# The closing work of each batch row, moved to other steps of the attention schedule (one core, Trainium2)

## The chip, the cores and the metric

The kernel runs on one core of one Trainium2 chip. The metric is the device time of one execution in microseconds, lower is better. The engines are named as the profile names them: PE is TensorE (matmuls and transposes), DVE is VectorE, ACT is ScalarE, POOL is GpSimd, SP is SyncE, which here only issues DMAs. All five run their own instruction streams in order and meet at semaphores only.

## The reference, cut to what matters

Four layers are computed one after the other on a tensor of 4 x 1024 x 256: a gated linear attention, a mixture of experts, a differential attention, and a second mixture of experts. Each is followed by a residual add and a layer norm. The change lies in the third layer:

```python
q1, q2 = (q[..., :hd], q[..., hd:])          # 16 heads of 16, two score maps each
s1 = jnp.einsum('bhqd,bhkd->bhqk', q1, k1) * scale
s2 = jnp.einsum('bhqd,bhkd->bhqk', q2, k2) * scale
a1 = jax.nn.softmax(causal s1);  a2 = jax.nn.softmax(causal s2)
out = jnp.einsum('bhqk,bhkd->bhqd', a1 - lam * a2, v)
rms = jnp.mean(out * out, axis=-1, keepdims=True)
out = out * jax.lax.rsqrt(rms + EPS) * head_norm_w * (1.0 - LAMBDA_INIT)
return out.transpose(0, 2, 1, 3).reshape(B, S, D) @ Wo.T + bo
...
x = _layernorm(x + _L1_attn_ref(x, ...), axis=-1)
```

So after the heads of one batch row b are done, what remains for that row is: square, mean over each head, inverse root, scale, transpose, one product with Wo, add to the residual x, and a layer norm. I call this the closing work of the row.

## The kernel before, in words

The attention stage (`attention`, L1735) handles 4 batch rows x 8 groups of two heads, 32 rounds `w` in all, with `b, g = w // 8, w % 8`. Every round has 24 steps `s`. What each engine does in a step is one string of letters in `STEPS` (L1776), and every engine walks the same generator `steps()` (L1806), picking out its own letters; so the order on each engine is fixed when the program is built. The letters that matter:

- `s`: scores of one block of keys, PE (L2359) into one of three single PSUM banks 4, 5, 6, two banks a step, then ACT's exponentials (L2063), one per bank. Blocks with few columns (steps 4, 6, 20, 22) pack two heads' maps in a bank, and the odd step after them has no scores.
- `m`: a part of the row maxima of a later round. PE (L2297, L2302) fills a pair of banks and DVE reduces it (L2158). Two bank pairs (0-1 and 2-3) take turns (`turn`, L1846). 19 of these a round, none in steps 1, 5, 6, 8, 15, 17 and 21 to 23.
- `v`: PE's products of exponentials and values (L2277).
- `h`, `H`, `d`: in step 4, PE transposes the heads of the round before (L2230) into one of the two bank pairs, ACT copies them out (L2102), and DVE takes the reciprocal of the denominators (L2108).
- `r`: in step 15, PE transposes the maxima (L2330), ACT copies them (L2040) and POOL splits them (L1985).
- `x`: POOL zeroes the upper triangle of a diagonal block (L1995), in steps 2, 7, 11 (twice), 21, 22, 23 (twice); the products of that block wait for it.
- `end`: the end of a step. The closing work of row b is spread over the ends of steps in the eight rounds after it, by small tables that map (round modulo 8, step) to a part. Row 3's closing work comes after the last round and is not governed by the tables.

The tables and what they place are these. `squared`: POOL squares one of eight parts (L1969), in steps 13 to 20 of round 0. `meant`: DVE's sums over heads (L2175), steps 18, 20, 22 of round 0 and step 0 of round 1. `all_squared`: ACT's inverse root of them (L80 and L82, `roots`), which waits for all four sums. `scaled`: POOL's multiplication of one of eight parts (L1974), which waits for the root. `joined`: PE transposes four blocks (L2312) into one single bank, ACT copies it (L2047). `put_out`: PE's fp32 product with Wo (L2323) into one single bank. `added`: DVE adds that bank to x (L2182) and takes the layer norm's statistics (L70, L74). `rooted`: ACT's inverse root of the variances (L80, L82). `normed`: DVE applies mean and root (L2195).

A part that needs a single bank takes the next of the three in turn, between the scores of the step before and the step after (`single`, L1841). PE writes the third bank after it only when its reader, ACT or DVE, has released it. In rounds 30 and 31 PE also multiplies weight matrices for the last layer (L2338) at the ends of steps 14 to 17 and 19 to 22 of round 30 and 5 to 8 and 12 to 15 of round 31, and DVE splits the results (L2169, L2171); there are no maxima of a later round left there.

The code rows around the tables:

Of the kernel before, what the change touches and what calls it, by code (L numbers as in the profile page):

```python
# [1734 lines left out]
def attention(nc, A, K, PS, D, own, before, keep):  # L1735
# [57 lines left out]
    exps_to = lambda m: first_exp[12] * (m // 12) + first_exp[m % 12]  # L1793

    biased = 14
    joined = {(1, 14): 0, (2, 3): 1, (2, 9): 2, (2, 15): 3}
    put_out = {(3, 14): 0, (4, 14): 1, (5, 14): 2, (6, 14): 3}
    added = {(3, 15): 0, (4, 15): 1, (5, 15): 2, (6, 15): 3}
    rooted = {(4, 19): 0, (6, 19): 1}
    normed = {(4, 23): 0, (5, 3): 1, (6, 23): 2, (7, 3): 3}  # L1800
    squared = {(0, 13 + i): i for i in range(8)}
    scaled = {(1, s): i for i, s in enumerate((5, 6, 8, 9, 13, 14, 15, 16))}
    all_squared = (1, 3)
    meant = {(0, 18): 0, (0, 20): 1, (0, 22): 2, (1, 0): 3}

    def steps():  # L1806
# [866 lines left out]
def program(nc, A, out):  # L2673
    with ExitStack() as ctx:
# [30 lines left out]
        st_rope = rope(nc, A, K, PS, D, own, st_moe)  # L2705
        late = ExitStack()
        st_att, parts = attention(nc, A, K, PS, D, own, st_rope, late)
        st_mix = mix(nc, A, K, PS, D, own, out, parts, late)
        stages = (st_gla, st_moe, st_rope, st_att, st_mix)
# [111 lines left out]
```

How the kernel before makes its waits and increments, by code:

```python
def clear(e, K, bank, stage):  # L49
    e.wait_ge(K.left, 5 * stage)
    n = [s.num for s in bank]
    e.sem_clear(range(n[0], n[-1] + 1)).then_inc(K.cleared, 1)
# [13 lines left out]
def layernorm_stats(e, step, ST, MV, tiles):  # L67
    for i, t in enumerate(tiles):
        n = step.on(e.bn_stats(ST[:, i, :], t))
        first = n if i == 0 else first
    for i in range(len(tiles)):
        e.wait_ge(step.sem, first + i)
        a = e.bn_aggr(MV[:, i, :], ST[:, i, :])
    return a
# [2 lines left out]
def rsqrt(e, step, K, dst, src, tmp, scale, col):  # L78
    n = step.on(e.activation(tmp, src, ACT.Ln, bias=K.EPS[:, col:col + 1], scale=scale))
    e.wait_ge(step.sem, n)
    return e.activation(dst, tmp, ACT.Exp, scale=-0.5)
# [69 lines left out]
    def sp(e, side):  # L152
# [13 lines left out]
        def weights(c):  # L166
            if c > 0:
                e.wait_ge(S.wplo, c)
            e.dma_start(WIN[:], A["we"][c // 2][:, 1536 * (c % 2):1536 * (c % 2) + 1536]).then_inc(S.g_ws, 16)
        def pairs(c):
            e.wait_ge(S.wplo, c + 1)
            for d, o in ((WPH, 0), (WPL, 3072)):
                e.dma_start(D.WP[c // 2][:, o + 1536 * (c % 2):o + 1536 * (c % 2) + 1536], d[:]).then_inc(S.g_wst, 16)
        weights(0)
        e.wait_ge(S.g_ld_out, 64)
        for d, n in ((D.XR[0:128, :], 256), (D.XN[0:128, 0:256], 256), (D.XN[0:128, 256:260], 4)):
            e.dma_start(d, GAM[:, 0:n]).then_inc(S.g_nst, 16)
        for t in range(9):
# [48 lines left out]
        def high(c):  # L229
            e.wait_ge(S.g_ws, 16 * (c + 1))
            if c > 0:
                e.wait_ge(S.g_wst, 32 * c)
```

## Time and profile before

| | before |
|---|---|
| median of 3 runs | 2290.94 us (2290.51 to 2291.24) |
| the profiled execution's own time | 2290.51 us |
| its span in the trace | 2288.8 us |
| PE busy over the span | 2137.9 us (93%) |
| DVE busy | 1569.5 us (69%) |
| ACT busy | 1236.7 us (54%) |
| POOL busy | 637.9 us (28%) |
| mean granted PE clock | 0.967 of 2.4 GHz |

The attention stage lies between about 1233 and 2063 us of the span. The shares above are averages over five stages; in this stage DVE, PE and ACT are all busy most of the time, and which one sets the pace is to be read step by step. I cut the stage into rounds at the start of DVE's first maximum of step 0; a round without closing work takes 23.3 us, and this repeats to a hundredth of a microsecond from round to round.

### The profile page before, as it was taken

What the parts mean: (1) busy time and instruction counts of PE and PEld (TensorE: products, weight loads), DVE (VectorE), ACT (ScalarE), POOL (GpSimd) and SP (SyncE); (2) the same over time, 40 slices, a digit from 0 to 9 for tenths busy, and PEclk for the clock granted to TensorE, in tenths of its full rate; (3) what the DMA queues carried; (4) which work ended last, traced back from release to release, by engine and by line L of the source; (5) the groups of instructions that cost most, each with busy time, mean ns of one, the idle gap of its engine ahead of it and who ended that gap; (6) DMA issues with size and microseconds to landing.
All of it is one profiled execution on the core that took longest, in us unless ns stands there. A gap on an engine that the chain in (4) does not pass through costs nothing.

```text
span 2288.8 us, 47120 instructions
## 1 busy us (share of the span) xinstructions
PE 2137.9 (93%) x17816; PEld 1331.3 (58%) x17816; DVE 1569.5 (69%) x2712; ACT 1236.7 (54%) x2379; POOL 637.9 (28%) x761
## 2 busy tenths in 40 slices
PE   7999999889999999995776999999999999999998
PEld 5888886556666666664654333344434434448886
DVE  3667767633333333336989899989999998946878
ACT  5767674213432233222331799888888888862110
POOL 1000000103333333333554243533343342322000
PEclk9999999999999999997887899999999999998999
DMA  4333335652222222223334010101111010200000
GB/s 141 130 105 129 110 101 196 214 202 34 53 38 36 36 38 38 37 34 133 127 143 141 30 64 31 40 33 51 35 38 51 32 42 30 71 20 7 22 19 28
DMA packets 90028, 163.77 MB, mean 72 GB/s; under 512 B 16225, under 2 KB 64353, under 8 KB 88145
## 3 DMA queue, kind: packets, MB, share of 16 engines
q1 hardware_dynamic: 76176, 141.98, 17.6%
q0 software_dynamic: 13632, 18.77, 5.0%
q8 instruction: 149, 2.44, 0.4%
q14 instruction: 71, 0.57, 0.1%
HBM read 99.70 MB, written 60.49 MB: 70 GB/s over the span
## 4 chain that ended last, share of the span: by engine, by line
PE 60%; DVE 14%; issue 2%; ACT 2%; DMA 1%; SPq 1%; POOL 0%; DVEq 0%; ACTq 0%
PE PS L2277 11%; PE PS L1446 8%; DVE NM L2158 7%; PE PS L58 6%; PE PS L60 6%; PE PS L59 6%; PE PS L2359 6%; PE PS L2302 5%; PE PS L1431 2%; DVE TT L1639 2%; DVE X L2549 2%; PE PS L2297 2%; PE PS L2230 1%; PE PS L2323 1%; DVE PP L1622 1%
## 5 line engine op out<-in xcount | busy, mean ns | idle before, releaser
L2158 DVE TENSOR_REDUCE NM<-PS 128x2 f32<-128x1024 f32 (+3 forms) x608 | 678.6, 1161 | 60.1 <-PE PS L2302 55.9
L2063 ACT ACTIVATE E<-PS 128x512 f32<-128x512 f32 (+2 forms) x1280 | 634.3, 554 | 115.0 <-PE PS L2359 105.8
L2277 PE MATMUL PS<-E,VP 128*32 128x256 f32 (+1 forms) x5120 | 364.7, 370 | 1.5 <-ACT OT L2095 1.1
L1243 DVE SCALAR_TENSOR_TENSOR XIL<-PS,XSC,XIH 128x128 f16<-128x128 f32 x142 | 43.3, 346 | 334.4 <-ACT XIH L1039 334.4
L1995 POOL TENSOR_SCALAR_AFFINE_SELECT E<-E 128x512 f32<-128x512 f32 x256 | 162.7, 637 | 290.5 <-ACT E L2063 290.5
L1074 ACT ACTIVATE HB<-PS 128x768 f32<-128x768 f32 x71 | 57.6, 811 | 300.8 <-PE PS L1431 300.8
L1446 PE MATMUL PS<-WALL,HB 128*128 x852 | 195.7, 379 | 1.0 <-ACT HB L1074 1.0
L2277 PEld LDWEIGHTS PS<-E,VP 128*32 128x32 f32 x5120 | 110.1, 109 | 147.8 <-issue 110.3
L2359 PE MATMUL PS<-QK 50*128 50x512 f16 (+3 forms) x1152 | 185.0, 332 | 4.2 <-DVE X L2182 2.1
L2302 PE MATMUL PS<-QK 48*128 48x512 f16 (+3 forms) x1152 | 172.7, 338 | 7.4 <-DVE NM L2158 7.4
L983 POOL DMA_INDIRECT XB<-x_normed,IDX x71 | 71.1, 1001 | 364.1 <-DVE GAT L1259 314.8
L1446 PEld LDWEIGHTS PS<-WALL,HB 128*128 128x128 f32 x852 | 156.5, 190 | 20.7 <-issue 2.4
L58 PE MATMUL PS<-WALL,XIH 128*128 x426 | 162.2, 381 | 6.1 <-issue 4.7
L59 PE MATMUL PS<-WALL,XIH 128*128 x426 | 162.2, 381 | 0.0
L60 PE MATMUL PS<-WALL,XIL 128*128 x426 | 162.0, 380 | 0.0
L2549 DVE SCALAR_TENSOR_TENSOR X<-PS,COMB,X 128x256 f32<-128x256 f32 x256 | 123.7, 483 | 21.7 <-PE PS L60 13.8
L2359 PEld LDWEIGHTS PS<-QK 50*128 50x128 f16 x1152 | 61.0, 94 | 124.2 <-ACT E L2063 102.3
L1552 POOL TENSOR_TENSOR TT<-TT 128x512 f32<-128x512 f32 x64 | 105.3, 1645 | 92.4 <-DVE TT L1639 91.5
L974 POOL DMA_INDIRECT x_resid<-YI,IDX x71 | 112.8, 1588 | 37.3 <-issue 19.7
L2297 PE MATMUL PS<-MR 64*128 64x64 bf16 (+2 forms) x1408 | 90.6, 208 | 25.1 <-DVE NM L2158 12.9
L2297 PEld LDWEIGHTS PS<-MR 64*128 64x128 bf16 x1408 | 50.6, 95 | 103.4 <-DVE NM L2158 66.1
L58 PE MATMUL PS<-CH,ZH 128*128 128x512 f32 x256 | 103.3, 404 | 3.0 <-DVE X L2549 3.0
(352 smaller groups left out, 3923.1 us busy)
## 6 DMA issues: line engine op xcount, KB each, us to landing
parts<-PP SPq DMA_DIRECT2D x32, 512.0 KB, 3.0
WIN<-in_we SPq DMA_DIRECT2D x16, 768.0 KB, 5.2
QK<-parts SPq DMA_DIRECT2D x96, 128.0 KB
WALL<-pairs_of_weights SPq DMA_DIRECT2D x7, 1536.0 KB
pairs_of_weights<-WPH SPq DMA_DIRECT2D x16, 384.0 KB, 2.4
pairs_of_weights<-WPL SPq DMA_DIRECT2D x16, 384.0 KB, 3.3
WALL<-in_we SPq DMA_DIRECT2D x8, 768.0 KB
QK<-parts SPq DMA_DIRECT2D x96, 64.0 KB
```

What stands on the lines that cost most here:

```text
L58: e.matmul(o, lh, rh, start=start, stop=False)
L59: e.matmul(o, lh, rl, start=False, stop=False)
L60: return e.matmul(o, ll, rh, start=False, stop=stop)
L1446: a = e.matmul(PS[:, b1 + 2, 0:256], HT[:, i, :], wide(r_last, 3072 + 256 * i, 256), start=i == 0, stop=i == 5)
L1995: e.affine_select(out=E[:, m % NE, :, 0:128], in_=E[:, m % NE, :, 0:128], pattern=[[0, 4], [1, 128]], compare_op=ALU.is_ge, fill=0.0, base ...
L2063: e.activation(dst, src, ACT.Exp, scale=unit).then_inc(S.ex, 1)
L2158: e.tensor_reduce(dst, src, AX, ALU.max).then_inc(S.mx, 1)
L2277: a = e.matmul(PS[32 * jj:32 * jj + 32, 7, 512 - n + c0:512 - n + c1], VP[b % 2][:, kt, 17 * hd:17 * hd + 32], E[:, m % NE, jj, c0:c1], st ...
L2297: e.matmul(PS[:, kb + x, 0:n * len(parts)].rearrange("p (z s) -> p z s", s=n)[:, :, c:c + 64], places[h][r, :], later[r, :].unsqueeze(1).t ...
L2302: a = e.matmul(PS[:, kb + x, n * z:n * z + n], q[r, y, 128 * i:128 * i + 128], k[r, y, c0:c0 + n], start=not masked, stop=True, skip_group ...
L2359: a = e.matmul(PS[:, kb, c:c + n], KS[w % 4][r, y, 128 * kt:128 * kt + 128], QS[w % 4][r, y, q0:q0 + n], start=True, stop=True)
L2549: a = e.scalar_tensor_tensor(out=X[:, t, :], in0=PS[:, product_bank(g), 256 * j:256 * j + 256], scalar=COMB[:, t, 2 * ep + j:2 * ep + j + ...
```

## The change

Only six tables of the attention stage change. No instruction is added or removed, and no size, buffer or engine changes.

```diff
     biased = 14
-    joined = {(1, 14): 0, (2, 3): 1, (2, 9): 2, (2, 15): 3}
-    put_out = {(3, 14): 0, (4, 14): 1, (5, 14): 2, (6, 14): 3}
-    added = {(3, 15): 0, (4, 15): 1, (5, 15): 2, (6, 15): 3}
-    rooted = {(4, 19): 0, (6, 19): 1}
-    normed = {(4, 23): 0, (5, 3): 1, (6, 23): 2, (7, 3): 3}
+    joined = {(1, 9): 0, (1, 15): 1, (2, 9): 2, (2, 15): 3}
+    put_out = {(3, 5): 0, (4, 5): 1, (5, 5): 2, (6, 5): 3}
+    added = {(3, 6): 0, (4, 6): 1, (5, 6): 2, (6, 6): 3}
+    rooted = {(4, 8): 0, (6, 8): 1}
+    normed = {(4, 9): 0, (5, 3): 1, (6, 9): 2, (7, 3): 3}
     squared = {(0, 13 + i): i for i in range(8)}
-    scaled = {(1, s): i for i, s in enumerate((5, 6, 8, 9, 13, 14, 15, 16))}
-    all_squared = (1, 3)
+    scaled = {(1, 2 + i): i for i in range(8)}
+    all_squared = (1, 1)
```

The following pieces are the difference in the order of the instructions; "-" rows stand there before, "+" rows after. On PE in round 11, the first with a product with Wo (L2323): L2230 are the head transposes of step 4, L2302 the maxima, L2359 the scores, L2277 the value products.

```order
 L2230 MATMUL PS<-IDN,OT 128x128 x8
 L2302 MATMUL PS<-QK 128x512 x2
+L2323 MATMUL PS<-WO,OB 128x256 x4
 L2359 MATMUL PS<-QS,KS 128x128 x4
 L2277 MATMUL PS<-E,VP 32x256 x4
...
 L2297 MATMUL PS<-MR 128x2x64 x4
 L2302 MATMUL PS<-QK 128x256 x4
-L2323 MATMUL PS<-WO,OB 128x256 x4
 L2359 MATMUL PS<-QS,KS 128x512 x2
 L2277 MATMUL PS<-E,VP 32x256 x4
```

The product moves from behind the maxima of step 14 to behind the maximum of step 4, ahead of the small scores of step 6.

On ACT in round 9: L2063 are the exponentials (512 wide in steps 0 and 1, 384 wide in 2 and 3), L2095 a copy of products, L80 and L82 the inverse root of the head sums.

```order
 L2063 ACTIVATE E<-PS 128x512 x4
-L2063 ACTIVATE E<-PS 128x384 x2
-L2095 ACTIVATE OT<-PS 128x512
-L2063 ACTIVATE E<-PS 128x384 x2
 L80 ACTIVATE ML<-MS,EPS 128x128
 L82 ACTIVATE MS<-ML 128x128
```

The root moves ahead of the exponentials of steps 2 and 3. On DVE in round 11, after the change: L2158 are the maxima, L2108 the reciprocal of step 4, L2182, L70 and L74 the add and the statistics, which stood behind the maximum "128x4" of step 14.

```order
 L2108 RECIPROCAL RC<-OH 128x32
 L2182 TENSOR_TENSOR X<-X,PS 128x512
 L70 BN_STATS ST<-X 128x6 x2
 L74 BN_AGGR MV<-ST 128x2 x2
 L2158 TENSOR_REDUCE NM<-PS 128x2 x3
```

The add now stands between the reciprocal of step 4 and the maximum of step 7.

## Rows read from the trace of the kernel before

**Rows 1.** Windows, cut at rounds: length, busy us (instructions) of PE, PEld, DVE, ACT, POOL, PE clock, DMA
```profile
1382.47:1405.78 23.31, 23.02 (x309) 9.10 (x309) 21.52 (x22) 21.15 (x45) 9.15 (x16) 1.00 0.10 36
1477.09:1502.86 25.77, 24.29 (x297) 9.59 (x289) 21.96 (x23) 21.35 (x46) 13.52 (x23) 0.93 0.09 33
1676.24:1700.49 24.25, 22.76 (x297) 8.88 (x289) 21.97 (x24) 21.29 (x46) 12.21 (x22) 1.00 0.10 35
1700.49:1725.57 25.08, 24.71 (x321) 10.58 (x321) 21.61 (x21) 22.58 (x48) 7.88 (x15) 1.00 0.10 34
1725.57:1750.40 24.83, 24.67 (x317) 10.45 (x317) 23.09 (x27) 21.17 (x45) 7.94 (x15) 1.00 0.19 63
1750.40:1775.87 25.47, 25.26 (x325) 10.66 (x325) 23.74 (x29) 22.03 (x48) 8.12 (x15) 1.00 0.14 52
1826.02:1849.17 23.15, 22.50 (x303) 8.87 (x301) 22.01 (x24) 20.57 (x44) 7.69 (x14) 1.00 0.11 37
```

**Rows 2.** Timeline of round 5, steps 4 to 9: start, us, instructions [idle before]
```profile
1388.08 0.28 PE L2359 MATMUL PS<-QK 50*128 50x128 f16 x4
...
1388.29 1.23 DVE L2158 TENSOR_REDUCE NM<-PS 128x2 f32<-128x1024 f32 x1 [0.70 <-PE PS L2302]
...
1388.86 0.39 PE L2302 MATMUL PS<-QK 48*128 48x512 f16 x2
...
1389.69 2.43 DVE L2158 TENSOR_REDUCE NM<-PS 128x2 f32<-128x1024 f32 x2
```

**Rows 3.** Timeline of round 19, steps 14 to 16: the product with Wo and the add
```profile
1739.99 1.99 PE L2323 MATMUL PS<-WO,OB 128*128 128x256 f32 x8
...
1741.91 0.39 PE L2359 MATMUL PS<-QS,KS 50*128 50x512 f16 x2
...
1742.03 0.68 DVE L2182 TENSOR_TENSOR X<-X,PS 128x512 f32<-128x512 f32 x1
...
1743.41 0.30 DVE L74 BATCH_NORM_AGGREGATE MV<-ST 128x2 f32<-128x6 f32 x2
...
1744.35 1.23 DVE L2158 TENSOR_REDUCE NM<-PS 128x2 f32<-128x1024 f32 x1 [0.63 <-PE PS L2302]
```

**Rows 4.** Timeline of round 17, steps 1 to 4: exponentials, last head sum, root, transposes
```profile
1675.90 1.09 ACT L2063 ACTIVATE E<-PS 128x512 f32<-128x512 f32 x2 [0.18 <-PE PS L2359]
...
1678.23 0.68 DVE L2175 TENSOR_REDUCE MS<-OB 128x32 f32<-128x512 f32 x1
...
1679.95 0.40 ACT L80 ACTIVATE ML<-MS,EPS 128x128 f32<-128x128 f32 x1
...
1680.38 0.31 ACT L82 ACTIVATE MS<-ML 128x128 f32<-128x128 f32 x1
...
1681.05 1.09 PE L2230 MATMUL PS<-IDN,OT 128*128 128x128 f32 x8
```

**Rows 5.** Timeline of round 18: the maximum behind the join of step 9
```profile
1711.22 0.96 DVE L2158 TENSOR_REDUCE NM<-PS 128x2 f32<-128x768 f32 x1 [0.48 <-PE PS L2302]
```

**Rows 6.** Timeline of round 20: root of the variances, step 19, and norm, step 23
```profile
1772.68 0.30 ACT L80 ACTIVATE LV<-MV,EPS 128x4 f32<-128x4 f32 x1
...
1775.13 0.81 DVE L2195 TENSOR_SCALAR X<-X,MV,RS 128x256 f32<-128x256 f32 x2
```

**Rows 7.** Timeline of round 30: the product of step 14, the scores of step 16
```profile
2013.22 1.89 PE L2323 MATMUL PS<-WO,OB 128*128 128x256 f32 x8
...
2019.19 0.39 PE L2359 MATMUL PS<-QK 50*128 50x512 f16 x2 [2.10 <-DVE X L2182]
```

**Rows 8.** Windows around the two falls of the PE clock, and the like of round 17
```profile
1477.60:1481.00 3.40, 2.02 (x36) 0.92 (x34) 3.40 (x5) 2.63 (x7) 0.64 (x1) 1.00 0.06 14
1481.10:1484.50 3.40, 3.40 (x22) 1.87 (x24) 1.52 (x2) 1.50 (x4) 2.87 (x5) 0.51 0.22 82
1675.70:1679.10 3.40, 2.70 (x48) 1.25 (x46) 3.40 (x6) 2.54 (x6) 0.64 (x1) 1.00 0.02 5
2016.90:2020.40 3.50, 1.40 (x13) 0.55 (x12) 2.95 (x7) 0.79 (x2) 0.55 (x2) 1.00 0.02 4
```

## The prediction, made before the changed kernel was run

> **What bounds the kernel now.** I read the windows cut at the rounds first, then the timeline of a round without closing work, then the timelines of the places that the change leaves and enters. A plain round takes 23.31 us and in it DVE is busy 21.52, ACT 21.15 and PE 23.02 us [rows 1]: three engines are nearly full, so there is little room for anything. The rounds with closing work tell what each part costs: 24.83 us with one product and add (round 19), 25.47 with product, add, root and norm (round 20), 24.25 with the root of the head sums and one join (17), 25.08 with three joins (18), and 23.15 in round 23, which carries only a norm in step 3 [rows 1]. So almost everything in the closing work is paid on the path today, and the question is only whether it is cheaper in the new places. The median of the runs, 2290.94 us, is 0.43 above the profiled execution's 2290.51, against which I add.
>
> **Product and add, step 14/15 to step 5/6 (12 times).** At step 14 the product is followed by the next scores 1.92 us after its start (1741.91 - 1739.99), the add and its statistics take DVE from 1742.03 to 1743.71, and then DVE still idles 0.63 us [rows 3]. The round grows by 24.83 - 23.31 = 1.52 us, less than 1.92, since PE would have waited there for an exponential anyway.
> At step 5, in a plain round, PE goes from the maximum of step 4 straight to the small scores (1388.08), and its maximum of step 7 starts at 1388.86; DVE starts its maxima of steps 4 and 7 at 1388.29 and 1389.69 [rows 2]. No engine waits for an exponential there, so nothing hides the product: PE is later by all of 1.92 us. On DVE the add can start 0.05 us behind the product's end, 1388.08 + 1.99 + 0.05 = 1390.12, and as the chain of the add occupies DVE for 1.59 us before the next maximum can start (1.68, less an overlap of 0.09), that maximum starts at 1391.71 in place of 1389.69: 2.02 later. A gap of 0.05 us in the next steps takes a little back; I take 1.95, between the two engines' figures. The empty steps 5 and 6 are empty of maxima, but DVE lags behind PE and uses them for the maximum of step 4. So each moved pair costs 1.95 - 1.51 = 0.44 us. For 11 of the 12 that is +4.8. Bounds: nothing, if the new place costs the same 1.51 (0), and 2.5 in place of 1.95 if the third scores behind it, which need the add's bank, also wait (+11).
>
> **The twelfth, in round 30.** There the product of step 14 stands between two weight products, and the scores of step 16 wait 2.10 us for the add that frees their bank, until 2019.19 [rows 7]. The product ends at 2015.11 and PE's wait begins at 2017.09 (2019.19 - 2.10), so 1.98 us of other work lie between. Without the product that work starts at 2013.22 and the scores of step 16 at about 2015.2, 4.0 us earlier. The product now costs 1.95 in step 5: net -2.0. Bounds: -1.9 for the product alone, if another reader keeps the bank, and -4.0 less 1.5.
>
> **Root of the head sums, step 3 to step 1 (3 times).** ACT ends the exponentials of step 1 at 1676.99. The last head sum is DVE's, from 1678.23 to 1678.91, in a queue of maxima that does not move. The root, 0.74 us long (1679.95 to 1680.69), now waits from 1676.99 to about 1678.96 and ends at 1679.70 [rows 4]. Behind it on ACT stand the exponentials of step 2, which today follow step 1's at once. They free the single banks: the second scores of step 3 can start at 1679.70 + 0.49 (one exponential) + 0.1 = 1680.3, the maximum of step 3, one value product and the scores of step 4 follow, the second of them behind another exponential, and the head transposes start at about 1681.85 in place of 1681.05 [rows 4]. DVE had work until then, so 2.7 us of delay become 0.8 on the path: +2.4 for three. Bounds: 0, if DVE's backlog covers it all, and 2.0 (all of ACT's wait) each, +6. On POOL five scales now stand ahead of the select of step 7; they start about 1 us earlier than today, and the product that needs the select comes behind the head transposes, so I cost them at nothing; if that cover failed it would be about 0.6 us a round.
>
> **Joins.** The three joins of round 18 cost 25.08 - 23.31 = 1.77, 0.59 each [rows 1], and the one at step 9 shows 0.57 of it (0.48 idle before the next maximum in place of an overlap of 0.09) [rows 5]. One goes from step 14 to 9, one from step 3 of round 18 to step 15 of round 17: they cost about the same anywhere, so +0.1 a row, +0.3 in all, with -0.3 and +1 as bounds.
>
> **Root of the variances and norm, steps 19/23 to 8/9 (6 times).** The norm holds DVE 0.81 us, 0.72 without the overlap [rows 6]; today round 20 pays 25.47 - 24.83 = 0.64 for it and round 23, with what is recovered after it, is 0.16 shorter than plain [rows 1], so 0.5. At step 9 ACT and DVE are both full, so I take 0.65: +0.15 for five, +0.65 for round 30, where step 23 cost nothing: +1.4. Bounds: -0.5 and +0.2 each.
>
> **Sum without the clock:** 4.8 - 2.0 + 2.4 + 0.3 + 1.4 = +6.9 us.
>
> **The clock.** In round 9 PE's clock falls from 2.4 to 1.2 GHz at 1481.1, after a stretch in which PE was busy 2.02 of 3.40 us, and the round is 25.77 - 24.25 = 1.52 us longer than round 17, the same work with 2.70 of 3.40 [rows 1, 8]. In round 30 it falls after the wait for the add, 1.40 of 3.50 busy [rows 8]; I put what comes back when the wait is gone at 1.3, a little under round 9's 1.5, as PE has waits there anyway. The root that waits adds over 1 us of idle PE to the very stretch of rounds 9, 17 and 25 that was near the edge, so I expect the clock to fall in two or all of these three: +1.5 or +3.0, I take +2.2.
> The Trainium skill (TensorE: Matmul & The Clock Gate, The HAM clock gate) says that the slow clock is the default and that activity keeps it away, so an idle wait is paid twice; the two falls here agree with it. Without that rule the sum would stay at +6.9.
>
> Together 6.9 - 1.3 + 2.2 = +7.8: 2290.51 + 7.8 = 2298.3 us. The likeliest case alone is 2295.5 to 2301.5.
>
> **Rivals.**
> *Nothing changes (2288 to 2294).* No instruction is added. If steps 5 and 6 hide product and add as well as step 14 did (0 in place of 4.8), the root's wait lies wholly under DVE's backlog and the clock keeps its falls, what is left is 1.51 - 4.0 for round 30, + 0.3 and + 1.4: about -0.8, 2289.7 us. For it: ACT and PE waits do not matter while DVE is busy. Against: the PE product has nothing to hide behind [rows 2].
> By the Trainium skill (Perfetto Trace Analysis, Identifying Performance Opportunities) it is the most contended engine's occupancy that matters; no engine's busy time changes, so the time would stay at 2290.5. The round of 24.83 us with DVE busy 23.09 speaks against reading it so here.
> *Faster (2283.7).* One mechanism: DVE waits 0.70 us before the maximum of step 4 [rows 2], because the head transposes hold one of two bank pairs. If a product directly behind lets PE run ahead again, so that the add fills such a wait, each pair costs 1.5 - 0.7 = 0.8: 11 x -0.7 = -7.7, round 30 0.8 - 4.0 = -3.2, and with the root, joins and norms (+4.1) this is -6.8. It decides where DVE, not PE, ends last behind the product. Against: the wait lies ahead of the product, not behind it.
> *Much slower (2302 to 2308).* The root's whole wait of 2.0 us reaches the path in three rounds (+3.6 over my value), and the scales ahead of the selects hold value products back by 0.6 in each (+1.8), and the clock falls in all three (+0.8): +14, 2304.5.
>
> **How the numbers follow.** The forecast has 0.67, nothing changes 0.14, faster 0.04, much slower 0.15. A difference under 0.2% (4.6 us) can't be told from none by a measurement of this kernel. The forecast's low end, 2295.5, is at that border, so a little of it goes to "same": faster 0.05, same 0.16, slower 0.79. The range, 2293.5 to 2303.5, reaches half into both neighbours.
>
> **What would show it.** Right: rounds 11, 19 and 27 about 25.25 us long (23.31 + 1.95), the maximum of step 7 starting some 3.4 us after that of step 4 in them, in place of 1.40, and the scores of step 16 of round 30 without a wait for DVE; ACT idle near 2.0 us before L80 in rounds 9, 17 and 25, and the head transposes 0.8 us later there; falls of the clock in two or three of these rounds and none at round 30. Wrong: rounds 11, 19 and 27 at 24.8 or less, or rounds 17 and 18 together no longer than 49.3 us. The forecast hangs most on the first.

## The result, and the profile after

The changed kernel takes 2302.76 us (median of 5 runs, 2300.73 to 2306.18), the kernel before 2291.24 in the same job (5 runs, 2290.51 to 2292.60). The ratio is 1.0052 with an interval of 1.0037 to 1.0066: 0.52% slower. The profiled execution took 2302.83 us with a span of 2301.1 us, 12.3 more than the span before. The page of the changed kernel, part 1 (busy us, share of the span, instructions):

```profile
span 2301.1 us, 47120 instructions
PE 2146.9 (93%) x17816; PEld 1335.8 (58%) x17816; DVE 1573.1 (68%) x2712; ACT 1236.4 (54%) x2379; POOL 636.5 (28%) x761
```

The instructions are the same. PE's busy time is 9.0 us more (2137.9 before), DVE's 3.6 (1569.5), the others' no more. Busy time also holds matmuls at the lower clock and instructions that stand still, so it does not tell where the 12.3 us came from, and the windows come first again. These are of the changed kernel, cut at the start of DVE's first maximum of step 0, with the columns of [rows 1] (length, busy us of PE, PEld, DVE, ACT, POOL, PE clock, DMA). They are rounds 5, 9, 12, 17, 18, 19, 20 and 23:

```profile
1383.63:1406.94 23.31, 23.02 (x309) 9.09 (x309) 21.52 (x22) 21.16 (x45) 9.12 (x16) 1.00 0.11 36
1478.27:1505.55 27.28, 24.98 (x301) 10.30 (x293) 22.06 (x23) 21.69 (x47) 13.47 (x23) 0.94 0.09 32
1555.40:1582.26 26.86, 25.23 (x317) 10.70 (x317) 24.65 (x29) 21.43 (x47) 9.11 (x16) 1.00 0.16 59
1682.45:1709.73 27.28, 24.98 (x301) 10.37 (x293) 22.13 (x23) 21.76 (x47) 12.17 (x22) 0.94 0.09 31
1709.73:1734.23 24.50, 24.12 (x317) 10.10 (x317) 21.62 (x22) 22.14 (x47) 7.91 (x15) 1.00 0.10 34
1734.23:1759.57 25.34, 25.05 (x317) 10.54 (x317) 23.13 (x26) 21.27 (x45) 7.86 (x15) 1.00 0.18 62
1759.57:1785.56 25.99, 25.23 (x317) 10.68 (x317) 23.78 (x29) 21.43 (x47) 7.86 (x15) 1.00 0.14 50
1836.89:1860.20 23.31, 23.02 (x309) 9.09 (x309) 22.17 (x24) 21.16 (x45) 7.90 (x15) 1.00 0.11 37
```

Against [rows 1]: the plain round is the same 23.31 to the hundredth, so nothing general happened. Round 19 (product and add) went from 24.83 to 25.34, and round 20 (with root and norm) from 25.47 to 25.99. Round 17 (root of the head sums) went from 24.25 to 27.28, and its clock column from 1.00 to 0.94. Round 18 lost a join and went from 25.08 to 24.50. Round 23 lost its little gain (23.15 to 23.31). Round 12 has the same closing work as round 20 and is 0.87 longer; before, both were 25.47.

**Product and add.** The timeline of round 19, steps 4 to 7, of the changed kernel (start, us, instructions, idle before):

```profile
1739.94 1.99 PE L2323 MATMUL PS<-WO,OB 128*128 128x256 f32 x8
1740.05 1.23 DVE L2158 TENSOR_REDUCE NM<-PS 128x2 f32<-128x1024 f32 x1 [0.70 <-PE PS L2302]
...
1741.87 0.28 PE L2359 MATMUL PS<-QS,KS 50*128 50x128 f16 x4
1741.97 0.69 DVE L2182 TENSOR_TENSOR X<-X,PS 128x512 f32<-128x512 f32 x1 [0.43 <-PE PS L2323]
1742.19 0.66 ACT L2063 ACTIVATE E<-PS 128x256 f32<-128x256 f32 x2 [1.84 <-PE PS L2359]
...
1743.58 1.19 DVE L2158 TENSOR_REDUCE NM<-PS 128x2 f32<-128x1024 f32 x1
```

The maximum of step 7 starts 3.53 us after that of step 4 (1743.58 - 1740.05); in [rows 2] it was 1.40. The small scores wait for all of the product, ACT idles 1.84 us for them, and DVE idles 0.43 before the add. Nothing hides the product here. In step 14 the same product ended with DVE idle 0.63 us and cost 1.52 [rows 1, 3]; here it costs 2.03.

**Root of the head sums.** Round 17, steps 1 to 4, which answers to [rows 4]:

```profile
1684.45 0.68 DVE L2175 TENSOR_REDUCE MS<-OB 128x32 f32<-128x512 f32 x1
1685.16 0.40 ACT L80 ACTIVATE ML<-MS,EPS 128x128 f32<-128x128 f32 x1 [1.97 <-DVE MS L2175]
...
1686.34 0.33 PE L2359 MATMUL PS<-QK 50*128 50x384 f16 x1 [0.97 <-ACT E L2063]
...
1688.12 1.11 PE L2230 MATMUL PS<-IDN,OT 128*128 128x128 f32 x4
```

ACT idles 1.97 us for the last head sum, 0.03 behind its end, and PE in turn 0.97 us for the exponential behind the root. The head transposes start 5.67 us after the round's start (1688.12 - 1682.45); before it was 4.81 (1681.05 - 1676.24). That is 0.86 later, and just there the clock falls:

```profile
1685.00:1688.00 3.00, 1.73 (x28) 0.63 (x22) 2.99 (x4) 2.72 (x7) 2.01 (x4) 1.00 0.19 49
1688.00:1691.40 3.40, 3.40 (x26) 2.05 (x22) 0.73 (x1) 2.23 (x5) 3.40 (x7) 0.50 0.25 94
```

PE ran at 2.4 GHz and was busy 1.73 of 3.00 us while it waited, and then ran at half speed with its queue full. The same occurs in round 9 (1483.2) and round 25 (1889.4). Of the two falls in the stage before, that of round 9 is still there and that of round 30 [rows 8] is gone.

**Norm and bias.** The norm's two halves in round 12 of the changed kernel, with the add of the bias on POOL, which by the table follows in step 14 and in time runs while DVE is at steps 9 and 10:

```profile
1566.84 1.28 POOL L1979 TENSOR_TENSOR X<-X,BO 128x512 f32<-128x512 f32 x1
1567.00 1.60 DVE L2195 TENSOR_SCALAR X<-X,MV,RS 128x256 f32<-128x256 f32 x2
1568.52 0.95 DVE L2158 TENSOR_REDUCE NM<-PS 128x2 f32<-128x768 f32 x1
```

and in round 20, where no bias is added:

```profile
1771.18 0.73 DVE L2195 TENSOR_SCALAR X<-X,MV,RS 128x256 f32<-128x256 f32 x2
```

The same two instructions take 1.60 us beside POOL's add and 0.73 without it. Taken one by one, the first half runs from 1567.00 to 1568.28 (1.27 us, 0.15 beyond the end of POOL's add) and the second takes 0.40. Rounds 12 and 14 both have this, which makes up the 0.87 between rounds 12 and 20.

**Round 30.** The product has left step 14 and the scores of step 16 come without a wait for DVE, against 2.10 us in [rows 7]:

```profile
2032.09 1.03 PE L2338 MATMUL PS<-WM 128*128 128x256 f32 x4
2033.06 0.39 PE L2359 MATMUL PS<-QK 50*128 50x512 f16 x2
```

From the start of round 30 to the end it is 287.84 us, after 290.62 before.

### The profile page after: what moved, and what is told of

The parts are those of the page before. It is cut to its first block, busy times and chain, and to the rows that moved or that the text cites. A ratio compares the mean times of both kernels' runs of the same rounds, so it can differ in the third digit from the quotient of the medians.

```text
span 2301.1 us, 47120 instructions
## 1 busy us (share of the span) xinstructions
PE 2146.9 (93%) x17816; PEld 1335.8 (58%) x17816; DVE 1573.1 (68%) x2712; ACT 1236.4 (54%) x2379; POOL 636.5 (28%) x761
## 4 chain that ended last, share of the span: by engine, by line
PE 59%; DVE 14%; ACT 3%; issue 2%; DMA 1%; SPq 1%; POOL 0%; DVEq 0%; ACTq 0%
PE PS L2277 11%; PE PS L1446 8%; DVE NM L2158 7%; PE PS L58 6%; PE PS L60 6%; PE PS L59 6%; PE PS L2359 6%; PE PS L2302 4%; PE PS L1431 2%; DVE TT L1639 2%; DVE X L2549 2%; PE PS L2297 2%; PE PS L2230 2%; ACT E L2063 1%; PE PS L2323 1%
## 5 line engine op out<-in xcount | busy, mean ns | idle before, releaser
L2158 DVE TENSOR_REDUCE NM<-PS 128x2 f32<-128x1024 f32 (+3 forms) x608 | 679.8, 1162 | 66.5 <-PE PS L2302 62.9
L2063 ACT ACTIVATE E<-PS 128x512 f32<-128x512 f32 (+2 forms) x1280 | 632.9, 555 | 120.5 <-PE PS L2359 112.6
L2277 PE MATMUL PS<-E,VP 128*32 128x256 f32 (+1 forms) x5120 | 364.8, 371 | 2.8 <-ACT OT L2095 2.0
L2277 PEld LDWEIGHTS PS<-E,VP 128*32 128x32 f32 x5120 | 110.0, 109 | 149.6 <-issue 107.8
L2359 PE MATMUL PS<-QK 50*128 50x512 f16 (+3 forms) x1152 | 190.7, 333 | 6.5 <-ACT E L2063 3.4
L2302 PE MATMUL PS<-QK 48*128 48x512 f16 (+3 forms) x1152 | 174.3, 339 | 7.4 <-DVE NM L2158 7.4
L2359 PEld LDWEIGHTS PS<-QK 50*128 50x128 f16 x1152 | 62.1, 94 | 130.5 <-ACT E L2063 110.2
```

Of the source, the lines that this page charges most:

```text
L2063: e.activation(dst, src, ACT.Exp, scale=unit).then_inc(S.ex, 1)
L2158: e.tensor_reduce(dst, src, AX, ALU.max).then_inc(S.mx, 1)
L2277: a = e.matmul(PS[32 * jj:32 * jj + 32, 7, 512 - n + c0:512 - n + c1], VP[b % 2][:, kt, 17 * hd:17 * hd + 32], E[:, m % NE, jj, c0:c1], st ...
L2302: a = e.matmul(PS[:, kb + x, n * z:n * z + n], q[r, y, 128 * i:128 * i + 128], k[r, y, c0:c0 + n], start=not masked, stop=True, skip_group ...
L2359: a = e.matmul(PS[:, kb, c:c + n], KS[w % 4][r, y, 128 * kt:128 * kt + 128], QS[w % 4][r, y, q0:q0 + n], start=True, stop=True)
```

## The experiments

The kernel before had medians of 2291.69, 2291.64 and 2292.51 us in the three jobs. A total carries some microseconds of clock falls that differ between executions of one kernel (its runs spread over 2 to 8 us), so each verdict goes by the length of single rounds, which repeat to about 0.01 us, and the total stands beside it. Where no interval is given there was one execution only. The round lengths of a kernel come from its one profiled execution; where the clock does not fall they agree between kernels with the same order, and whether it falls in a given round can differ from one execution to the next.

**a_product_only**: before, with the product and the add of the change alone.

```diff
-    put_out = {(3, 14): 0, (4, 14): 1, (5, 14): 2, (6, 14): 3}
-    added = {(3, 15): 0, (4, 15): 1, (5, 15): 2, (6, 15): 3}
+    put_out = {(3, 5): 0, (4, 5): 1, (5, 5): 2, (6, 5): 3}
+    added = {(3, 6): 0, (4, 6): 1, (5, 6): 2, (6, 6): 3}
```

> The kernel before with only the product with Wo and its add moved to steps 5 and 6. Theory (the product has nothing to hide behind there, and PE and DVE work one after the other): each of the 11 ordinary rounds grows from +1.51 to +2.03 us over a plain round, +5.7 in all; round 30 gives back 4.0 for the scores that no longer wait and 1.3 for the fall of the clock at 2020, and pays 2.03; sum +2.4 us, about 2293.6. Rival (the moved product costs no more than at step 14, and what made the changed kernel slower lies in the root alone): -3.8 us, about 2287.4.

Measured: 2293.44 us, ratio 1.0008 (0.9998 to 1.0017). Round 19:

```profile
1727.66:1753.00 25.34, 25.05 (x317) 10.54 (x317) 23.12 (x27) 21.27 (x45) 7.89 (x15) 1.00 0.18 64
```

It is 25.34 us, the same as with the whole change, so the pair's price is its own. The clock fell neither in rounds 9, 17, 25 nor in round 30, and from round 30 on it took 287.04 us, 3.6 less than before. The pairs' 11 x 0.52 = +5.7, round 9's fall -1.5, round 30 and after -3.6, and the start of round 1, which was 1.5 later, give +2.1; the span grew by 2.1 (2290.9).

**b_root_only**: before, with the root and the scales of the change alone.

```diff
-    scaled = {(1, s): i for i, s in enumerate((5, 6, 8, 9, 13, 14, 15, 16))}
-    all_squared = (1, 3)
+    scaled = {(1, 2 + i): i for i in range(8)}
+    all_squared = (1, 1)
```

> The kernel before with only the root of the head sums at step 1 and POOL's scales in steps 2 to 9. Theory (ACT waits 1.97 us for the last head sum, of which 0.83 reach the path, and the idle PE brings the clock down in rounds 17 and 25 as well as 9): +2.5 and +3.0, about 2296.8 us, with the head transposes 0.8 us later in rounds 17 and 25 before the clock is counted. Rival (ACT's wait is covered by DVE's backlog, no fall is added): 2291.2.

Measured: 2296.91 us, ratio 1.0025 (1.0016 to 1.0035). Round 17:

```profile
1677.86:1702.95 25.09, 23.00 (x297) 9.01 (x289) 21.96 (x24) 21.11 (x46) 12.21 (x22) 1.00 0.10 33
```

Its clock did not fall here, and it is 0.84 over the 24.25 of [rows 1]: this is the wait alone. Rounds 9 and 25, where it fell, were longer than a plain round by 3.29 and 3.28, so a fall adds 1.5 (3.28, less 25.09 - 23.31 = 1.78). The two prices of the root are told apart.

**c_root_back**: the changed kernel, with only the root back in step 3.

```diff
-    all_squared = (1, 1)
+    all_squared = (1, 3)
```

> The changed kernel with only the root of the head sums back at step 3; the scales stay in steps 2 to 9 and so wait for it on POOL. Theory (the root's wait on ACT is the cause, and it brings two of the three falls of the clock): -2.5 for the wait and -3.0 for two falls, 2297.3 us, ACT without an idle time before L80. Rival (the early scales, which stand ahead of the select of step 7 on POOL, are the cause): no gain, since they now start later still, 2302.8 or more.

Measured: 2297.86 us, ratio 1.0024 (1.0014 to 1.0034), close to the expected total, but by another way. No fall came in rounds 9, 17 and 25, and the round was not cheap all the same (round 17, then POOL and PE in it):

```profile
1680.84:1707.46 26.62, 23.39 (x301) 9.46 (x293) 22.05 (x23) 21.79 (x47) 12.17 (x22) 1.00 0.09 32
```

```profile
1685.38 2.94 POOL L1974 TENSOR_TENSOR OA<-OA,MS 128x256 f32<-128x256 f32 x5 [3.09 <-ACT MS L82]
1688.27 0.63 POOL L1995 TENSOR_SCALAR_AFFINE_SELECT E<-E 128x512 f32<-128x512 f32 x1
...
1688.95 0.86 PE L2277 MATMUL PS<-E,VP 128*32 128x256 f32 x16 [0.66 <-POOL E L1995]
```

Five scales wait for the root and stand ahead of the select of step 7, which starts 7.43 us after the round's start (before, where two stand ahead of it, 5.69). The value product behind it waits 0.66 us for POOL, and against [rows 1]'s round 17 the maximum of step 9 comes 0.73 us late and that of step 10 another 1.50, in place of the root's 0.83 at step 4 and the join's 0.57 at step 10. In this round the kernel differs from j_join_only (below, 24.94) only in the place of the scales, so with the root in step 3 the early scales cost 1.68 us, against 0.84 for the root in step 1. So the wait that I expected to win back was not won back; it changed its place and grew. In the profiled execution the gain was in the falls (three of about 1.5 us), and in the clock behind the stage: from round 30 on it took 282.98 us, 4.9 less than the changed kernel. That last part is not the edit's, as j_join_only shows.

**i_scales_back**: the changed kernel, with the scales back in their old steps.

```diff
-    scaled = {(1, 2 + i): i for i in range(8)}
+    scaled = {(1, s): i for i, s in enumerate((5, 6, 8, 9, 13, 14, 15, 16))}
```

> The changed kernel with POOL's scales back in steps 5, 6, 8, 9 and 13 to 16 of round 1; the root stays at step 1. Theory (five scales ahead of the select of step 7 are covered and cost nothing): round 17 shows the same extra time at the maximum of step 4 (+0.83, and +1.5 where the clock falls), and the same +0.56 at step 10. Rival (the scales hold the selects, and through them the value products, back): rounds 9, 17 and 25 get 0.6 us shorter each.

Measured: 2303.2 us. Round 17:

```profile
1682.88:1710.16 27.28, 24.97 (x301) 10.36 (x293) 22.06 (x24) 21.78 (x47) 12.34 (x22) 0.94 0.09 31
```

It is the same 27.28. With the root in step 1 the early scales cost nothing, as the prediction had it; they only do with the root in step 3, as c_root_back shows (1.68 us).

**j_join_only**: before, with the joins of the change alone.

```diff
-    joined = {(1, 14): 0, (2, 3): 1, (2, 9): 2, (2, 15): 3}
+    joined = {(1, 9): 0, (1, 15): 1, (2, 9): 2, (2, 15): 3}
```

> The kernel before with only the joins moved, to steps 9 and 15 of rounds 1 and 2. Theory (a join costs much the same at steps 3, 9, 14 and 15): rounds 17 and 18 together grow by 0.1 us. Rival (the join of step 9 of round 1 now waits for the fourth scale, which POOL ends late as the root is at step 3): +0.5 us or more in round 17.

Measured: 2287.92 us. Rounds 17 and 18, and all from round 30 to the end:

```profile
1678.15:1703.09 24.94, 23.23 (x301) 9.45 (x293) 22.07 (x24) 21.80 (x47) 12.20 (x22) 1.00 0.09 34
1703.09:1727.63 24.54, 24.17 (x317) 10.13 (x317) 21.62 (x21) 22.15 (x47) 7.94 (x15) 1.00 0.10 34
2000.34:2286.20 285.86, 272.07 (x1607) 203.06 (x1607) 206.60 (x478) 74.42 (x156) 34.42 (x49) 0.98 0.06 21
```

The two rounds are 49.48 together, 0.15 more than the 49.33 before, and rounds 25 and 26 are 0.09 more: the joins move their cost and hardly change it. The third row is the surprise. The same stretch of the kernel before:

```profile
1998.18:2288.80 290.62, 277.10 (x1607) 207.48 (x1607) 206.47 (x478) 74.58 (x156) 34.43 (x49) 0.97 0.06 20
2071.60:2085.30 13.70, 13.70 (x54) 12.33 (x55) 2.90 (x4) 4.08 (x7) 5.25 (x8) 0.50 0.01 1
```

It has the same instructions from here on (x1607, x478, x156, x49) and is 4.76 us longer. Behind the attention stage PE works through 13.70 us at 1.2 GHz with its queue full; in j_join_only this stretch is 3.4 us long (from 2096.4). Nothing in the edit touches it. In the fourteen traces the time at 1.2 GHz behind the stage comes in two sizes whatever the edit: 13.6 to 13.7 us in nine, the changed kernel's among them, and 3.4 us in five (c_root_back, g_half_after, h_half_before, this one and l_filler).

**e_norm_back**: the changed kernel, with root and norm back in steps 19 and 23.

```diff
-    rooted = {(4, 8): 0, (6, 8): 1}
-    normed = {(4, 9): 0, (5, 3): 1, (6, 9): 2, (7, 3): 3}
+    rooted = {(4, 19): 0, (6, 19): 1}
+    normed = {(4, 23): 0, (5, 3): 1, (6, 23): 2, (7, 3): 3}
```

> The changed kernel with the root of the variances and the norm back at steps 19 and 23. Theory (the norm costs 0.64 at step 9 and 0.65 less 0.14 recovered in the next round at step 23, nothing in round 30, and in rounds 12 and 14 another 0.87 since POOL's bias add holds it up): -0.6 -0.65 -1.7 = -3.0 us, about 2299.8. Rival (moved root and norm cost the same as before, 0 us): 2302.8.

Measured: 2297.49 us, ratio 1.0024 (1.0011 to 1.0037). Round 12:

```profile
1555.71:1581.69 25.98, 25.64 (x325) 10.75 (x325) 23.77 (x28) 22.12 (x48) 9.31 (x16) 1.00 0.16 58
```

It is 25.98 in place of 26.86, and round 13 won 0.14: the collision with the bias and the lost recovery are both gone, 0.87 twice and 0.14 five times. The total fell further than the 2299.8 expected; the trace cannot say why, as its own execution (span 2298.5) had a longer fall in round 9 (6.8 us) and lay above the median.

**d_bias_late**: the changed kernel, with the bias in step 18.

```diff
-    biased = 14
+    biased = 18
```

> The changed kernel with POOL's add of the bias (L1979) at the end of step 18 in place of 14. In the changed kernel the norm at step 9 takes 1.27 us for its first half in rounds 12 and 14, where that add runs on POOL at the same time, and 0.41 in rounds 20, 22, 28 and 30. Theory (the two instructions cannot run side by side, and the second waits for the first): both norms take 0.41 + 0.40 us, rounds 12 and 14 shrink by 0.87 each, -1.7 us, about 2301.1. Rival (the first batch row is slow for another reason, the data or the residual's placement): 1.27 us stays, 2302.8.

Measured: 2302.34 us, ratio 1.0045 (1.0028 to 1.0062): no gain. The norm of round 12, and rounds 12 and 16:

```profile
1565.37 0.73 DVE L2195 TENSOR_SCALAR X<-X,MV,RS 128x256 f32<-128x256 f32 x2
```

```profile
1553.77:1579.76 25.99, 25.24 (x317) 10.68 (x317) 23.76 (x29) 21.43 (x47) 9.13 (x16) 1.00 0.15 58
1654.39:1680.04 25.65, 24.14 (x329) 9.72 (x333) 23.21 (x25) 22.25 (x47) 13.91 (x24) 1.00 0.10 34
```

and in round 16 the bias on POOL and what waits:

```profile
1672.13 1.27 POOL L1979 TENSOR_TENSOR X<-X,BO 128x512 f32<-128x512 f32 x1
1673.37 1.75 POOL L1969 TENSOR_TENSOR OB<-OA 128x256 f32<-128x256 f32 x3
1675.07 1.21 POOL L1995 TENSOR_SCALAR_AFFINE_SELECT E<-E 128x512 f32<-128x512 f32 x2
```

```profile
1675.75 0.64 PE L2277 MATMUL PS<-E,VP 128*32 128x256 f32 x8 [1.17 <-POOL E L1995]
```

The two halves take 0.73 us and round 12 is as long as round 20 (25.99), so POOL's add is what held the norm. But round 16 was 24.70 us before and is 25.65 now, and round 8 too: the bias now stands among the four squares (L1969) ahead of a select, and the value products wait 1.17 us for that. Two times 0.87 won, two times 0.95 lost. The mechanism held and the edit was a bad cure.

**g_half_after** and **h_half_before**: the changed kernel and the one before, each with half of the contraction of the product with Wo left out, so that they compute something else.

```diff
-                for k in HALF:
+                for k in (0,):
```

> The changed kernel with half of the product with Wo left out in the first three batch rows (one of the two contraction halves; 0.95 us of PE less in each of 12 places). Theory (at step 5 the product on PE and the add on DVE stand one behind the other, and with a short product the add still takes DVE 1.59 us behind the reciprocal): rounds 11, 19 and 27 fall from +2.03 to about +1.5 over a plain round, -6 us in all. Rival (PE alone is what the product delays): to +1.1, -11 us.

> The kernel before with the same half of the product left out. Theory (at step 14 DVE is behind PE, so that the add starts at the same time as with a whole product and ends its 1.59 us, of which 0.71 lie in an idle time that a plain round has too): rounds 11, 19 and 27 fall from +1.51 to about +0.8 to +0.9. Rival (PE alone): to +0.55.

Measured: 2292.84 and 2283.83 us. Round 19 of the first, then of the second:

```profile
1733.53:1758.28 24.75, 24.38 (x313) 9.82 (x313) 22.96 (x27) 21.26 (x45) 7.89 (x15) 1.00 0.19 64
```

```profile
1725.94:1750.51 24.57, 23.87 (x313) 9.69 (x313) 23.08 (x27) 21.29 (x45) 7.94 (x15) 1.00 0.22 73
```

From the product's start to the next scores PE now takes 1.06 us in place of 1.93, 0.87 less. In steps 5/6 that takes 0.59 us from the round (25.34 to 24.75): DVE no longer idles before the add, and its own add and statistics stay. In step 14 it takes only 0.26 (24.83 to 24.57), where I expected 0.6 to 0.7 and the rival 0.96: both missed. The trace of the second shows what takes over:

```profile
1742.40 0.68 DVE L2182 TENSOR_TENSOR X<-X,PS 128x512 f32<-128x512 f32 x1
1743.13 0.39 PE L2359 MATMUL PS<-QS,KS 50*128 50x512 f16 x2 [0.54 <-DVE X L2182]
```

and the same scores in round 19 of the kernel before:

```profile
1743.02 0.39 PE L2359 MATMUL PS<-QS,KS 50*128 50x512 f16 x2
```

With half a product the scores of step 16 wait for the bank that the add reads, and the add stands behind a maximum of step 14. With the whole product they start without a wait, 0.31 us after the add's end (1742.71), so there the product's length sets the 1.52 us; what h_half_before shows is that only 0.26 of it could be saved before the add's place in DVE's queue takes over.

**f_round30_only**: before, with the product of round 30 alone in step 5.

```diff
-                    yield w, s, "end", (w % 8, s)
+                    yield w, s, "end", (w % 8, {5: 14, 6: 15, 14: 5, 15: 6}.get(s, s) if w == 30 else s)
```

> The kernel before with only the twelfth product and add moved to steps 5 and 6, those of round 30; the other eleven stay at step 14 and 15. Theory (only this one gains from the move, as the scores of step 16 no longer wait for the add and the clock does not fall behind that wait): -4.0 + 2.03 - 1.3 = -3.3 us, about 2288.0 beside 2291.2. Rival (the gain of round 30 is given back by the weight products around it): 2291.

Measured: 2285.70 us, ratio 0.9972 (0.9960 to 0.9985). Its six runs lie between 2281.37 and 2289.80. This one of the twelve pairs is worth moving. The scores of step 16 start 19.14 us after the round's start in place of 21.01. In the profiled execution (span 2287.2) the clock fell once more before the stage ended (at 2033.4, 35 us behind that round's start), and from that round on it took 288.8 us, 1.8 less than before.

**k_add_at_14**: before, with the add one step earlier. It changes DVE's order in round 30 alone, where it comes ahead of the copy of the weight product.

```diff
-    added = {(3, 15): 0, (4, 15): 1, (5, 15): 2, (6, 15): 3}
+    added = {(3, 14): 0, (4, 14): 1, (5, 14): 2, (6, 14): 3}
```

> The kernel before with the add at the end of step 14 in place of 15. On DVE this changes the order in round 30 alone: the add stands ahead of the split of the first weight product and no longer behind it. Theory (the bank of the product was held by the add, which stood behind a split that waited for PE): the scores of step 16 start 2.1 us earlier, at once behind the weight product, the clock does not fall there (-1.3): -3.4 us, about 2287.9. Rival (PE is late there for its own work): 2291.2.

Measured: 2283.25 us, ratio 0.9967 (0.9955 to 0.9978), the lowest median of all and faster than both kernels. Round 30, steps 14 to 16:

```profile
2013.73 1.89 PE L2323 MATMUL PS<-WO,OB 128*128 128x256 f32 x8
...
2015.66 0.69 DVE L2182 TENSOR_TENSOR X<-X,PS 128x512 f32<-128x512 f32 x1 [1.56 <-PE PS L2323]
...
2017.53 0.39 PE L2359 MATMUL PS<-QK 50*128 50x512 f16 x2
```

The product stays where it was, the add follows it at once, and the scores of step 16 start 18.84 us after the round's start in place of 21.01, without a wait. The bank was kept by the place of its reader in DVE's queue and not by the product. The clock did not fall, and from round 30 on it took 287.01 us, 3.6 less than before. The median won 8.4 (2283.25 against 2291.64), the span of the profiled execution 3.1. Its seven runs fall in two groups, 2281.82 to 2283.25 and 2286.25 to 2287.63, and the profiled one (2287.49) is of the longer, with 13.6 us at 1.2 GHz behind the stage. The shorter group may be executions with 3.4 us there, but no trace of one is kept, so where the rest was won stays open. f_round30_only and this one are not told apart by their intervals.

**l_filler**: the changed kernel, with six matmuls repeated ahead of the scores of step 3 in rounds 9, 17 and 25, into a bank that they overwrite anyway.

```diff
+                    for _ in range(6 if w in (9, 17, 25) and s == 3 and x == 0 else 0):
+                        e.matmul(PS[:, kb, c:c + n], KS[w % 4][r, y, 128 * kt:128 * kt + 128], QS[w % 4][r, y, q0:q0 + n],
+                                 start=True, stop=True)
```

> The changed kernel with six more matmuls on PE in each of rounds 9, 17 and 25, which write the first score bank of step 3 again with the same values, while PE waits there for ACT's exponential (1.2 us idle, 1.0 us of it filled). Theory (the clock falls in these rounds because PE stands idle in that wait, and each fall costs 1.5 us): none or one of the three falls is left, and the rounds shrink to +2.5 over a plain round: -3 to -4.5 us, 2298.3 to 2299.8. Rival (the falls have another cause, or the additional matmuls cost their own time): 2302.8 or more.

Measured: 2298.96 us, ratio 1.0037 (1.0023 to 1.0052), as expected. The fillers, and rounds 9 and 17:

```profile
1688.39 1.14 PE L2360 MATMUL PS<-QK 50*128 50x384 f16 x6
```

```profile
1478.97:1507.44 28.47, 27.42 (x307) 11.05 (x299) 22.31 (x24) 21.77 (x47) 13.52 (x23) 0.88 0.09 30
1685.80:1711.56 25.76, 24.43 (x307) 10.10 (x299) 22.06 (x24) 21.60 (x47) 12.21 (x22) 1.00 0.09 33
```

Round 17 is 1.52 shorter than with the change (27.28) though PE has 1.14 us more to do, and round 25 is 25.77 in place of 27.19. In round 9 it fell nevertheless, for longer (clock 0.88), and a further fall came in round 12 (1571.7). One execution of three rounds would show little, since the fall of round 9 comes and goes without any edit near it (there before and in k_add_at_14, not in a_product_only and f_round30_only, whose order up to there is the same). The traces together show more. With the root in step 1 (the changed kernel, b_root_only, d_bias_late, e_norm_back, g_half_after, i_scales_back) the clock fell in 16 of 18 of the rounds 9, 17 and 25; with the root in step 3 (the kernel before and the six other kernels) in 2 of 21; with the root in step 1 and the fillers in 1 of 3. So the root's new place brings the falls. That PE's idle time is how it does so fits the fillers, with three rounds to go by, and filling one wait is no cure that holds. e_norm_back had the same long fall in round 9 (28.48 us) without fillers.

## Why the prediction was right, point by point

The forecast was 2298.3 us with a range to 2303.5; 2302.76 lies in it, 0.7 below its upper end. It lies in the window of my rival "much slower" too, and nearer to that one's 2304.5 (1.7 us) than to my own value (4.5 us), so that the range held owes something to luck. The direction and the mechanisms of the forecast showed in the trace, with sizes near those that I gave (the pairs 0.9 us over, the falls 0.7); what I lacked were two terms, and one of them is no effect of the change. By steps, in us of the profiled executions:

| step | predicted | measured |
| --- | --- | --- |
| eleven moved pairs | +4.8 (0.44 each) | +5.7 (0.52 each: 2.03 - 1.51) |
| round 30 to the end | -2.7 (-2.0, norm +0.65, clock -1.3) | -2.8 |
| root of the head sums | +2.4 (0.8 each) | +2.5 (0.83 each, b_root_only) |
| joins | +0.3 | +0.3 (0.09 to 0.15 each, j_join_only) |
| norm of five rounds | +0.75 | +0.7 (0.14 each) |
| falls in rounds 17 and 25 | +2.2 | +2.9 (1.5 and 1.4) |
| norm beside POOL's bias | not seen | +1.7 (0.87 twice) |
| start of the stage | not seen | +1.2 |
| sum | +7.8 | +12.2, span +12.3 |

- **The pairs** were the step on which most hung, and it held: rounds 11, 19 and 27 are 25.34 (I said about 25.25), the maximum of step 7 comes 3.53 us after that of step 4 (I said 3.4). The 0.08 that was missing each time lies on DVE: I let 1.95 stand between PE's 1.92 and DVE's 2.02 and gave 0.05 back for a gap that is not there; the round grew by 2.03, DVE's own figure. g_half_after shows that both engines have a share.
- **Round 30** went as said: no wait at step 16 and no fall, and the time at 1.2 GHz behind the stage was 13.7 us in both traces, so the -2.8 is not of its making. But the cause was narrower than I put it. k_add_at_14 shows that the add's place behind the weight product's copy kept the bank, and that the gain was to be had without moving the product: from round 30 on it took 287.01 us with the product left in step 14, a_product_only 287.04 with it moved.
- **The root**: ACT's idle 1.97 (said 2.0), the transposes 0.86 later (said 0.8), b_root_only 0.84 in all. The rival of its whole 2.0 on the path is out.
- **The scales** cost nothing where the change puts them (i_scales_back). The price of 0.6 for a failed cover was too small: in c_root_back, where they hold the select, they cost 1.68.
- **The clock** fell in all three rounds, the upper of my two cases. A fall costs 1.5 us in rounds 9 and 17 and 1.4 in round 25. The sixteen of eighteen under l_filler say that three was the likelier number; the 2.2 that I took stood for one or two added ones.
- **The step that failed** is the norm's. Its price held where no bias is added, and in rounds 12 and 14 another 0.87 each came on top, which my sum had at nothing. I priced its new place by DVE and ACT being full and did not ask what POOL does there. In rounds 12 and 14 it is the add of the bias, and the first half of the norm takes 1.27 us in place of 0.40: it ends at 1568.28, 0.15 after POOL's add (1568.13). d_bias_late and e_norm_back both take the 0.87 away. The Trainium skill (SBUF — State Buffer, Who interferes with whom) states that a DVE instruction in one of the two-port modes, which a tensor_scalar can enter, and a GpSimd instruction exclude each other: the one that issues first keeps the shared port pair for its whole length and the other one blocks. The traces agree, with POOL's add first by 0.16 us and the norm at 1.60 beside it and 0.73 without it; in which mode the norm ran no trace shows.
- **Start of the stage**: round 1 began 1.2 us later than before. With the same work ahead of it, it began at 1289.6 in c_root_back and 1289.7 in e_norm_back, which have tables of the change, and at 1292.7 in j_join_only and 1289.4 before. So it varies between executions (1289.4 to 1292.7 over the fourteen traces), and no effect of the change is shown.

Of the rivals, "nothing changes" fell with a_product_only (the pairs cost 0.52 each), and "faster" with the 0.43 us that DVE idles before the add. "Much slower" came nearer in time than the forecast did, but by mechanisms that mostly did not occur: the root's wait cost 0.84 and not 2.0, the scales nothing, and only its third fall came.

## What to carry to other kernels

Empty steps in a table aren't idle engines: look at what each in-order engine does at that time, and above all whether the work put there keeps the next scores waiting. Before a product is moved because its bank comes free late, look where the bank's reader stands in its own queue; here moving the reader one step earlier made the kernel 0.33% faster (0.9967), while moving all twelve products and adds made no difference that the runs can tell (1.0008, 0.9998 to 1.0017). When an elementwise instruction is moved on DVE, look at what POOL does in the same microseconds.

## What the runs showed of the hardware that I had not expected

- A DVE normalization of 128x256 took 1.27 us while POOL added 128x512, and 0.40 alone; the wait is in the instruction's own duration, no idle time shows it.
- 1607 matmul records with the same work took 285.86 us or 290.62, by a stretch at 1.2 GHz behind the stage that was 3.4 or 13.7 us long. What sets its length stays open, and it alone is 0.2% of the kernel's time.
- A fall of the clock in the dense part costs 1.4 to 1.5 us. In the same three rounds it came 16 times of 18 with the root's wait and 2 times of 21 without it; with the wait and 1.14 us of repeated matmuls in it, once of 3. With the same wait it came in rounds 9 and 25 and not in 17 (b_root_only), so the wait makes a fall likely and does not fix it.
